# Moving the router's scales in a two-phase mixture-of-experts kernel: one power for both scales of a part, two parts' scales put between sends, constants loaded over ScalarE's queue

## What is computed

```python
x = x + 0.5 * ffn(layernorm(x))
x = x + attn(layernorm(x))
x = x + 0.5 * ffn(layernorm(x))
```

```python
r_in = x * rsqrt(mean(x**2) + 1e-6) * d**-0.5 * router_scale
logits = r_in @ router_w
top_k_idx = top_k(logits, 2)            # weights from the softmax of the two
gate0, gate1 = x @ gating_w[:, 0], x @ gating_w[:, 1]   # 256 hidden, per expert
out = sum over the two experts of weight * ((gelu(gate0) * gate1) @ linear_w)
```

## Time and profile before

| | us |
|---|---|
| median of 3 runs | 640.43 (637.59 to 641.42) |
| the profiled execution, its own time | 640.15 |
| its span | 638.1 |
| PE busy in the span | 520.2 |
| POOL busy in the span | 363.3 |
| first send starts on POOL | 26.27 |
| last of the 56 sends starts | 97.34 |

### The profile page before, as it was taken

The page is one execution under the profiler, slowest core; times in us unless marked ns, Lnnn a source line. Parts: engine busy times, 40 slices in busy tenths (PEclk is TensorE's granted clock), DMA queues, the critical chain, the costliest instruction groups (busy, mean ns, idle before and its releaser), DMA issues.

```text
span 638.1 us, 20679 instructions
## 1 busy us (share of the span) xinstructions
PE 520.2 (82%) x7242; PEld 457.1 (72%) x7243; DVE 416.4 (65%) x1431; ACT 277.3 (43%) x627; POOL 363.3 (57%) x425
## 2 busy tenths in 40 slices
PE   0899865999999599999999899999730999999920
PEld 0666635899999478888788778878520999999920
DVE  5776653666676857677688887656324566766747
ACT  0444112443443246666566657555420344434404
POOL 8777775775566431343657565561667556656630
PEclk9999896999999679999899999999855899999975
DMA  9611222222322312010212111120102222323259
GB/s 268 206 48 54 68 70 51 84 71 83 83 82 75 100 51 66 23 52 20 76 30 76 35 40 33 44 55 19 34 27 77 72 81 85 83 74 92 83 143 277
DMA packets 60136, 49.37 MB, mean 77 GB/s; under 512 B 8736, under 2 KB 53536, under 8 KB 59936
## 3 DMA queue, kind: packets, MB, share of 16 engines
q1 hardware_dynamic: 51872, 31.51, 18.6%
q0 software_dynamic: 8192, 16.86, 8.0%
HBM read 23.55 MB, written 20.59 MB: 69 GB/s over the span
## 4 chain that ended last, share of the span: by engine, by line
PE 57%; DVE 13%; POOL 10%; issue 8%; DMA 5%; ACT 3%; SPq 3%; DVEq 0%; POOLq 0%; ACTq 0%
PE PS L560 16%; PE PS L574 7%; PE PS L634 7%; POOL xs_rows L408 6%; PE PS L628 5%; DVE MB L1278 4%; DVE X L1250 4%; PE PS L526 3%; PE PS L549 3%; PE PS L782 2%; POOL ys_rows L423 2%; PE PS L818 2%; DMA XS<-xs_rows 2%; PE PS L624 2%; DMA ys_rows<-YO,XS 1%
## 5 line engine op out<-in xcount | busy, mean ns | idle before, releaser
L423 POOL DMA_INDIRECT ys_rows<-YO,XS x136 | 130.9, 963 | 89.5 <-issue 54.5
L560 PE MATMUL PS<-XST,WG 128*128 128x128 f32 x1088 | 151.3, 283 | 0.0
L408 POOL DMA_INDIRECT xs_rows<-XN,IDX x120 | 118.0, 984 | 36.2 <-issue 34.1
L560 PEld LDWEIGHTS PS<-XST,WG 128*128 128x128 f32 x1088 | 134.9, 195 | 3.9 <-issue 0.2
L1179 DVE TENSOR_TENSOR AV<-PS,GA 128x256 f32<-128x256 f32 x136 | 57.7, 424 | 85.5 <-PE PS L574 43.1
L1278 DVE TENSOR_REDUCE MB<-PS 128x8 f32<-128x1024 f32 x64 | 78.2, 1222 | 42.7 <-PE PS L624 42.4
L893 ACT ACTIVATE GA<-PS 128x256 f32<-128x256 f32 x136 | 52.1, 383 | 95.7 <-PE PS L560 95.5
L574 PE MATMUL PS<-EXP,AV 128*128 x544 | 83.2, 276 | 1.3 <-DVE AV L1179 1.2
L628 PE MATMUL PS<-QM,K 32*128 32x128 f32 x1024 | 76.8, 287 | 5.8 <-DVE MB L1278 4.2
L922 ACT ACTIVATE PT<-PS 128x1024 f32<-128x1024 f32 x64 | 64.4, 1022 | 31.0 <-PE PS L624 17.4
L634 PE MATMUL PS<-MOP,PICKS 32*128 32x128 f32 x1024 | 74.7, 287 | 0.9 <-issue 0.8
(11 more groups left out here) (172 smaller groups left out, 882.0 us busy)
## 6 DMA issues: line engine op xcount, KB each, us to landing
XS<-xs_rows SPq DMA_DIRECT2D x136, 64.5 KB, 1.8
VM<-VM SPq DMA_DIRECT2D x32, 128.0 KB, 2.4
XN<-ys_rows SPq DMA_DIRECT2D x16, 256.0 KB, 5.4
YG<-ys_rows SPq DMA_DIRECT2D x14, 256.0 KB, 2.8
EXP<-experts SPq DMA_DIRECT2D x1, 3072.0 KB, 11.2
ys_rows<-YO,XS POOLq DMA_INDIRECT x136, 2.2
X<-x SPq DMA_DIRECT2D x4, 512.0 KB, 6.3
xs_rows<-XN,IDX POOLq DMA_INDIRECT x120
```

The lines of the kernel that those rows point to most:

```text
L408: pool.indirect_dma_start(xs, bass.IndirectOffsetOnAxis(ap=IDX[:, place, c, i:i + 1], axis=0), XN[:, c, place, i, :], None).then_inc(scatt ...
L423: pool.indirect_dma_start(ys, bass.IndirectOffsetOnAxis(ap=XS[:, r, D:D + 1].bitcast(U32), axis=0), YO[:, r, :], None).then_inc(ys_out[r], 16)
L560: ins = pe.matmul(HPS[r % 2][:, c * P:(c + 1) * P], WG[r % 2][:, c * P:(c + 1) * P], XST[r % 2][:, :], start=True, stop=True)
```

## The change

- POOL makes both scales of a part by one power of 128x2x8 (`BOTH[1] = BOTH[0] ** -0.5`). The second input is now 1e-6 * vareps + v, made by one more instruction on DVE in `part_stats`, and stok is put together on DVE by two products (`part_logit_scales`).
- POOL makes the scales of parts 0 and 1 ahead of the sends, those of part 2 after the first group's eight sends and those of part 3 after the second group's.
- DVE takes the statistics of part 2 after `first_route(0)` and those of part 3 after `first_route(1)`. The shifts of part 2 (which wait for POOL's power of part 2) stand just ahead of that, and those of part 3 after `first_route(3)`. The constants are prepared after the statistics of part 0.
- ACT issues CN, RS and RW (semaphore c_loaded) and the nine other arrays (w_loaded); SP issues EXP right after x, and PICKS later. The product with WO moves on PE from its first place to the step k = 1.

```diff
+        BOTH = [sb(f"BOTH{i}", [P, 2, T]) for i in range(2)]
+        ALL["vareps"], ALL["rstd"] = BOTH[0][:, 0, :], BOTH[1][:, 0, :]
...
-            for dst, src in ((CN, consts), (RS, rscale), (RW, rw), (PES, pes), (WQ, wq), (WK, wk), (WV, wv),
-                             (BQ, bq), (BK, bk), (BV, bv), (BO, bo)):
-                sp.dma_start(dst[:, :], src).then_inc(w_loaded, 16)
-            sp.dma_start(WO[:, :], wo).then_inc(w_loaded, 16)
-            sp.dma_start(PICKS[:, :], picks).then_inc(picks_loaded, 16)
             sp.dma_start(EXP[:, :], experts).then_inc(e_loaded, 16)
...
             def part_scales(h):
                 pool.wait_ge(var_ready, h + 1)
-                router_scales(ALL, part_tiles(h), h)
-
-            for h in range(PARTS):
-                part_scales(h)
+                at, n = part_tiles(h), T // PARTS
+                pool.tensor_tensor(BOTH[1][:, :, at], BOTH[0][:, :, at], NHALF[:, 0:2 * n].rearrange("p (k t) -> p k t", k=2),
+                                   ALU.pow).then_inc(rstd_ready, 1)
+
+            part_scales(0)
+            part_scales(1)
...
                 route(k, g)
+                if k < 2:
+                    part_scales(2 + k)
...
-            pe.wait_ge(bv_spread, 1)
-            pe.matmul(M1[:, 0:D], BVB[:, :], WO[:, :], start=True, stop=True).then_inc(bvo_done, 1)
...
+                if k == 1:
+                    pe.wait_ge(w_loaded, 16 * WEIGHT_LOADS)
+                    pe.wait_ge(bv_spread, 1)
+                    pe.matmul(M1[:, 0:D], BVB[:, :], WO[:, :], start=True, stop=True).then_inc(bvo_done, 1)
...
+            for dst, src in ((CN, consts), (RS, rscale), (RW, rw)):
+                act.dma_start(dst[:, :], src).then_inc(c_loaded, 16)
+            for dst, src in ((PES, pes), (WQ, wq), (WK, wk), (WV, wv), (BQ, bq), (BK, bk), (BV, bv), (BO, bo)):
+                act.dma_start(dst[:, :], src).then_inc(w_loaded, 16)
+            act.dma_start(WO[:, :], wo).then_inc(w_loaded, 16)
...
+            def part_logit_scales(h):
+
+                at = part_tiles(h)
+                dve.wait_ge(rstd_ready, h + 1)
+                step(dve.tensor_tensor(ALL["stok"][:, at], ALL["vareps"][:, at], ALL["rstd"][:, at], ALU.mult))
+                dve.tensor_tensor(ALL["stok"][:, at], ALL["stok"][:, at], BOTH[1][:, 1, at], ALU.mult).then_inc(stok_ready, 1)
...
-            for h in range(PARTS - 1):
-                part_stats(h)
-            dve.wait_ge(w_loaded, 16 * WEIGHT_LOADS)
-            dve.tensor_copy(BVB[:, :], BV[:, :].broadcast_to([P, P])).then_inc(bv_spread, 1)
+            part_stats(0)
+            dve.wait_ge(c_loaded, 16 * 3)
             region_starts()
...
+            part_stats(1)
             first_rows(0)
             first_rows(1)
-            part_stats(PARTS - 1)
-
-            for h in range(PARTS - 1):
-                part_shifts(h)
+            part_logit_scales(0)
+            part_shifts(0)
+            part_shifts(1)
             for k in range(GROUPS):
                 first_route(k)
                 if k == 0:
+                    part_logit_scales(1)
+                    part_stats(2)
+                    dve.wait_ge(w_loaded, 16 * WEIGHT_LOADS)
+                    dve.tensor_copy(BVB[:, :], BV[:, :].broadcast_to([P, P])).then_inc(bv_spread, 1)
+                if k == 1:
                     dve.wait_ge(bvo_done, 1)
                     dve.tensor_tensor(BO[:, :], BO[:, :], M1[:, 0:D], ALU.add).then_inc(bo_ready, 1)
-                if k == 1:
-                    part_shifts(PARTS - 1)
+                    part_shifts(2)
+                    part_logit_scales(2)
+                    part_stats(3)
+                if k == 3:
+                    part_shifts(3)
+                    part_logit_scales(3)
                 dense_rows(k)
```

More of the change, by code:

```diff
@@ L207, in macaron @@
         x_loaded = [sem(f"x_loaded{h}") for h in range(PARTS)]
+        c_loaded = sem("c_loaded")
         w_loaded, e_loaded, xs_zeroed = sem("w_loaded"), sem("e_loaded"), sem("xs_zeroed")
@@ L246, in macaron @@
         stored, groups_sent, tiles_sent = sem("stored"), sem("groups_sent"), sem("tiles_sent")
-        WEIGHT_LOADS = 12
+        WEIGHT_LOADS = 9
         def tiles(g, n=TG):
@@ L291, in _ @@
             sp.dma_start(xs[E * REGION:ROWS, :].rearrange("(n p) d -> p n d", p=P), FILL[:, E:, :]).then_inc(xs_zeroed, 16)
+            sp.dma_start(PICKS[:, :], picks).then_inc(picks_loaded, 16)
             def row_at(reg, entry, high):
@@ L802, in attend @@
                     to_tokens(i - 2)
-            pe.wait_ge(w_loaded, 16 * WEIGHT_LOADS)
             pe.wait_ge(consts_set, 1)
-            pe.wait_ge(bv_spread, 1)
-            pe.matmul(M1[:, 0:D], BVB[:, :], WO[:, :], start=True, stop=True).then_inc(bvo_done, 1)
             rows_bank, logits_bank, prefixes_bank = ROUTER
@@ L1352, in part_stats @@
                     step.later(dve.bn_stats(BST[:, i, :], X[:, tiles_of_part.start + i, :]))
-                moments(ALL, tiles_of_part).then_inc(var_ready, 1)
+                moments(ALL, tiles_of_part).then_inc(dve_step, 1)
+                step.n += 1
+                step.wait()
+                dve.scalar_tensor_tensor(out=BOTH[0][:, 1, tiles_of_part], in0=ALL["vareps"][:, tiles_of_part], scalar=RMS_EPS,
+                                         in1=ALL["var"][:, tiles_of_part], op0=ALU.mult, op1=ALU.add).then_inc(var_ready, 1)
             def first_rows(k):
```

## The result

The changed kernel takes 651.2 us (median of 4 runs, 649.3 to 653.9) against 639.2 us (637.6 to 641.4) of the kernel before on the same chip: ratio 1.0194, interval 1.0164 to 1.0224, so it is slower by 12 us. The profiled execution took 652.0 us, with a span of 650.0 and a mean granted clock of 0.911 (before 0.920).

What follows compares the result with a forecast made beforehand. The prediction took POOL's sends to bound the front: -2.5 (first send) + 10.5 (second group) + 2.8 (fourth power) + 1.0 (group 4) - 0.7 (clock) = +11.1 on 640.15, so 651.3 us; range 647 to 656 for 8 in 10.

Steps and rivals of the forecast that it cites:

- What bounds it: Front of the kernel: POOL's sends set its length, by when the first starts and what is put between them.
- The first send: POOL's first send at 23.7 us, 2.5 earlier (1.9 to 4.0), with x landing 1.5 later beside CN.
- The second group's sends: POOL's ninth send: DVE and POOL wait crosswise, 21.7 us from the first send instead of 11.26, 10.5 lost.
- The fourth power: On POOL between the second and third groups' sends: 2.8 us lost (1.5 to 3.2).
- Group 4: Fifth group in order: DVE waits for the fourth power, PE behind it, so its sends lose 1.0 us (0 to 2).
- The end of the dense chain: Last dense sum at 112.7 us, still hidden behind the sends at 114.7, by 2 us only.
- The clock: TensorE at the first slots may still run at 2.4 GHz: a gain of 0.7 us, at most 1.5.
- The range: Whole kernel: bounds from the terms together +7.3 (647.5) to +14.5 us (654.7); 647 to 656 for 8 in 10.
- Late weights: Rival: ACT's first copy waits for the last weight, delaying the first send; 652.5 to 658.5 us; chance 0.10.
- No crossing: Rival: group 2's places are ready when POOL wants them, only two powers cost; +3.1, 643.3 us; chance 0.06.
- Not slower: Rival: the first send's head start pays for what is put between sends; -0.9, 639.2 us; chance 0.04.

Runs made afterwards that it cites:

- the three variants on the last chip: The change uncrossed, then also with the third power in POOL's idle time, then also with reordered loads: 645.99, 641.03, 640.86 us; kernel before 639.94.
- the second profile of the change: The change unaltered, run again on another chip: median 651.69 us against 639.94 before, ratio 1.0158; this profiled execution took 656.5 us.
- b4_experts_last: The changed kernel with constants issued after x's first part lands and prepared after part 1's statistics, EXP issued after all constants and weights: ratio 1.0137 to kernel before.
- f3_power_in_idle: The changed kernel, uncrossed by earlier part 2 and 3 statistics, third power in POOL's idle time before the first send: 641.03 us, ratio 1.0019 to kernel before.
- a4_late_constants: The changed kernel with constants issued after x's first part lands, prepared after part 1's statistics, ACT's wait for weights later: ratio 1.0281 to kernel before.
- f2_uncrossed: The changed kernel with part 2's shifts and products and part 3's statistics on DVE moved behind group 2's routing: 645.99 us, ratio 1.0077 to kernel before.
- all eight on the two slower chips: First eight follow-up runs, variants of the change or of the kernel before, on chips where the kernel before takes 723.7 or 713.1 us: ratios 0.998 to 1.0281.

## Why the prediction was right, step by step

**What bounds it**, the sends: right for the profiles of before, of the change's first and of the three variants on the last chip; in the second profile of the change it was the dense chain. First send, gap, powers and last send carry the loss, and moving the sends back moved the time back.

**The first send**: 24.47 instead of 23.7, so 1.8 earlier, not 2.5, which is 0.1 outside its bounds (1.9 to 4.0). The term that was off is x's landing: 7.32, 2.2 later than before, where I took 1.5 by an even split and had 2.1 as the other end. The rest of the path came as stated: the first send is 9.81 us behind the first transposes at 14.66, 9.84 before. That CN overtakes x is shown by CN's 4.4 us and by `b4_experts_last`, where x lands at 5.03 as soon as CN waits for it. The Trainium skill, "DMA: Bandwidth & Descriptors", section on queues, rings and completion order, has each DMA engine take turns between queues by packets; I worked out from it that CN's 5.6 KB rows go nearly first and that the term is 2.1. The trace (2.2) agrees with that and not with my even split.

**The second group's sends**: predicted 21.7 from first to ninth, measured 21.42; +10.2 against 11.26. The parts came as named: eight sends and power end at 37.45, LGS at 40.79, IDX at 44.82 to 45.04. Taking the crossing away made it 14.24. This is shown. The loss by the wait alone is 7.2 of the 10.2, the power itself the other 3.

**The fourth power**: predicted 2.8, measured 58.92 - 45.89 = 13.03 against 10.21, 2.8.

**Group 4**: predicted 1.0, measured 1.4 (70.47 - 58.92 = 11.55 against 10.10 to 10.21). DVE's second wait was 2.20 us, not 5 and more as I had written: PE's dense step at 47.76 took 3.76 us at the granted clock of 0.50, against 2.05 for the same step at 105.41 at 1.00, and DVE was late by then (IDX at 56.26). So the time went partly to PE's slow step and partly to the wait; no run separates the two.

**The end of the dense chain**: predicted 112.7 and hidden by 2 us; its last sum ended at 115.43 in the first profile, level with the slots, and at 119.6 in the second. Here the prediction was too sure. I priced one slow step. The granted clock fell to 0.50 several times: in both profiles around 44 to 50, 60 to 64 and 80 to 82 us, in the first again at 98 to 100, in the second at 90 to 92 and 106 to 112. The spread of 6.5 us between the runs of the change is no evidence for it, since the kernel before spreads by 8.1.

**The clock**: the -0.7 did not show. In the first profile the clock fell to 0.50 at 118 to 120 us all the same, and the seventh slot came 8.54 us behind the second (before 8.51). How much there was to gain the runs do show: in `f3_power_in_idle` and in the second profile of the change the clock was 1.00 there, and the same stretch took 7.24 and 7.21, 1.3 us less, close to my upper end of 1.5. The terms as measured make -1.8 + 10.2 + 2.8 + 1.4 = +12.6 at the last send, and some slower sends near 98 us (1.46 and 1.27 instead of 0.96) the rest of +13.3. My terms without the clock made +11.8, so the front was 1.5 too small. Behind it I expected 0.7 back from the clock; 1.6 came back by 224 us (1.4 by the end), and not from the clock but at the 13th and 24th slots, for whose rows PE waited 0.94 us each before and 0 and 0.58 after. The loss was 12.0 by the medians and 11.9 by the spans, against 11.1; 651.3 lies so near 651.2 because the median of before in these runs was 639.2, 1.0 below the 640.15 that I had started from. That the forecast meets the median to 0.1 is luck; its single terms were off by up to 0.7, the front in all by 1.5.

**The range**: the bounds of the terms as I stated them add up to +5.2 and +14.1 when all fall on one side, not to +7.3 and +14.5. The measured +12.0 lies within either.

**The rivals.** Late weights: ACT in order of time, the changed kernel:

```profile
13.23 0.20 ACT L995 ACTIVATE BQS<-BQ 128x1 f32<-128x1 f32 x1 [4.69 <-DMA WO<-wo]
15.85 0.58 ACT L879 COPY XNT<-PS 128x512 f32<-128x512 f32 x1 [2.42 <-PE PS L521]
```

WO landed at 13.2, and the first copy at 15.85 waited for PE's transposes and not for it. The trace refutes the rival for this kernel. Its premise, EXP issued ahead of WO, did not hold (7.25 against 6.74). Where it does hold, in `a4_late_constants`, even a 4 KB constant took 14.3 us beside EXP. No crossing is refuted by the row at 45.89, and `f2_uncrossed` shows what it would have cost: 6.05 us over before and not my 3.1, since the head start was 1.7 and not 2.5, and the wait ahead of the 25th send was missing from it. Not slower is refuted by the time.

## What to carry to other kernels

If engine A waits for a result that stands in engine B's program behind a long queue of work, look at what B will want next from A: if it is made behind that same wait, the two queues take turns instead of overlapping, and the price is the whole round trip, not the one instruction. Move the wait behind what the other engine needs next, or put the small work where that engine idles anyway (here 8 us ahead of the first send). A second load queue is no free start: here what went on it displaced the first queue's transfers (x landed 2.2 us later), and a small load issued behind the start of a large one waited long for it. And look for every chain behind the same wait: here it held up PE's dense steps along with the sends.

## What the runs showed that I had not expected

- A load of 4 KB took 14.3 us when a 3 MB load with 24 KB rows had been issued 1.0 us ahead of it on the other queue, 6.5 when the large one was issued 5.6 us behind it, and 6.9 with the large one held back. Part of the 14.3 is CN ahead of it in its own queue (10.7 instead of 7.2). Holding x free of CN gained 2.2 to 2.6 us at its landing and at most 0.3 at the first send once EXP was held back too.
- The power on POOL took 1.64 us for 8 columns, 2.93 for 16 and 4.83 for 28: the 16 of two halves with a stride lie on the line of the other two.
- Which of two nearly level chains ends the front depends on the chip and the execution: the sends in the profiles of before and of three variants and in one of the change, the dense chain in the other of the change and in all eight on the two slower chips.
